# The 48-row group of up products moved to the front in a stage of eight experts, and ScalarE's loop over the experts written out

## What is computed

```python
gate_up = jnp.einsum('ecd,edm->ecm', buf, w_up_gate)
gate, up = jnp.split(gate_up, [I], axis=-1)          # I = 176
h = jax.nn.silu(gate) * up
out_buf = jnp.einsum('eci,eid->ecd', h, w_down)
```

## Time and profile before

| | us |
|---|---|
| median of 3 runs | 791.88 |
| lowest and highest | 791.78, 792.73 |
| the profiled execution | 792.51 |
| its span, in which all profile times lie | 790.5 |
| PE, DVE, ACT, POOL busy | 739.8, 574.6, 467.8, 544.3 |

### The profile page before, as it was taken

The page is one execution under the profiler, slowest core; times in us unless marked ns, Lnnn a source line. Parts: engine busy times, 40 slices in busy tenths (PEclk is TensorE's granted clock), DMA queues, the critical chain, the costliest instruction groups (busy, mean ns, idle before and its releaser), DMA issues.

```text
span 790.5 us, 14041 instructions
## 1 busy us (share of the span) xinstructions
PE 739.8 (94%) x4364; PEld 628.5 (80%) x4364; DVE 574.6 (73%) x1539; ACT 467.8 (59%) x1163; POOL 544.3 (69%) x459
## 2 busy tenths in 40 slices
PE   5799999999999999999999999999899989899993
PEld 4587788888888888888777888777778879888882
DVE  6976886777777766868887777988754447777577
ACT  5567776676666676765666766665633246554262
POOL 4466998787878887777888888778534253431773
PEclk9999999999999999999999999999999999999997
DMA  9411245422222212222222221212142035441352
GB/s 299 124 53 54 84 158 180 156 72 72 63 68 66 74 61 69 62 67 58 65 65 83 82 80 61 63 58 64 48 152 71 34 139 199 176 166 67 88 149 84
DMA packets 47748, 75.73 MB, mean 96 GB/s; under 512 B 9728, under 2 KB 24640, under 8 KB 47680
## 3 DMA queue, kind: packets, MB, share of 16 engines
q1 hardware_dynamic: 43504, 65.19, 26.6%
q0 software_dynamic: 3072, 8.39, 3.4%
q10 hardware_dynamic: 1104, 1.31, 0.5%
HBM read 57.71 MB, written 17.17 MB: 95 GB/s over the span
## 4 chain that ended last, share of the span: by engine, by line
PE 71%; DVE 11%; issue 8%; ACT 4%; POOL 3%; DMA 2%; DVEq 0%; ACTq 0%; POOLq 0%
PE ps L433 20%; PE ps L969 16%; PE ps L934 13%; PE ps L985 9%; PE ps L955 7%; PE ps L1133 3%; POOL got L1883 1%; DVE q_sw L1315 1%; DVE q_sw L1314 1%; DVE hid_both L1646 1%; POOL slot_inputs L1790 1%; DVE hid_hi L1636 1%; POOL o_lo L1774 1%; DVE hid L1641 1%; DVE hid L1633 1%
## 5 line engine op out<-in xcount | busy, mean ns | idle before, releaser
L969 PE MATMUL ps<-pt,vp 128*128 128x512 f32 (+3 forms) x512 | 149.5, 434 | 10.3 <-DVE q_sw L1315 10.0
L634 ACT ACTIVATE prob<-ps,neg_max 128x512 f32<-128x512 f32 (+3 forms) x256 | 132.6, 525 | 34.7 <-DVE neg_max L1324 30.6
L969 PEld LDWEIGHTS ps<-pt,vp 128*128 128x128 f32 x512 | 82.7, 190 | 59.9 <-issue 30.5
L1324 DVE CUSTOM_DVE_ANT_0 ps<-ps,causal_row 128x512 f32<-128x512 f32 (+3 forms) x256 | 120.1, 511 | 5.5 <-PE ps L934 5.4
L1755 POOL TENSOR_TENSOR q_sw<-q_cos,q_sw 128x512 f32<-128x512 f32 x62 | 79.2, 1277 | 64.4 <-DVE q_cos L1316 64.3
L643 ACT ACTIVATE pt<-ps,vcol 128x512 f32<-128x512 f32 x64 | 44.1, 690 | 109.5 <-PE ps L955 109.5
L1774 POOL TENSOR_TENSOR o_lo<-o_t,o_hi 128x512 fp32r<-128x512 f32 x64 | 84.3, 1317 | 33.4 <-ACT o_hi L672 33.4
L955 PE MATMUL ps<-id_f,prob 128*128 128x128 f32 x640 | 92.3, 275 | 0.9 <-ACT pt L643 0.9
L934 PE MATMUL ps<-k_hi,q_hi 128*128 128x512 f32 x248 | 87.1, 351 | 0.4 <-POOL q_lo L1759 0.3
L1759 POOL TENSOR_TENSOR q_lo<-q_sw,q_hi 128x512 fp32r<-128x512 f32 x62 | 80.2, 1293 | 4.0 <-ACT q_hi L666 3.6
L1343 DVE TENSOR_TENSOR o_t<-ps,inv_row 128x512 f32<-128x512 f32 x64 | 44.3, 692 | 52.5 <-PE ps L969 52.5
(11 more groups left out here) (220 smaller groups left out, 1940.2 us busy)
## 6 DMA issues: line engine op xcount, KB each, us to landing
kh_row<-kvh_rows SPq DMA_DIRECT2D x64, 256.0 KB, 3.2
inv_row<-inverse_sums SPq DMA_DIRECT2D x64, 256.0 KB, 3.2
slot_inputs<-zeros SPq DMA_DIRECT2D x8, 640.0 KB, 4.9
xg<-slot_inputs SPq DMA_DIRECT2D x8, 640.0 KB, 4.5
slot_outputs<-yo SPq DMA_DIRECT2D x8, 640.0 KB, 3.3
up_raw<-in_w_up_dram SPq DMA_DIRECT2D x8, 368.0 KB, 4.8
wo_raw<-in_wout_dram SPq DMA_DIRECT2D x4, 512.0 KB, 7.9
dn_sb<-in_w_dn_dram SPq DMA_DIRECT2D x8, 256.0 KB, 3.7
```

Source lines behind the costliest of these rows:

```text
L634: ins = act.activation(prob[:, i % 2, ROW_AT[nt]:ROW_AT[nt] + w], ps_s[bank][:, at:at + w], ACT.Exp, scale=-1.0, bias=neg_max[:, i % 2, nt ...
L969: ins = pe.matmul(ps_qo[:, mt * P:SEQ], vp[:, b * TPB + mt, :], pt[:, i % 2, cols], start=(mt == 0), stop=(mt == PT_BANKS[-1][-1]))
L1324: ins = dve.tensor_tensor_reduce(s_, s_, causal_row[:, (NT - 1 - nt) * P:], 1.0, BIG, ALU.add, ALU.min, neg_max[:, i % 2, nt:nt + 1])
```

## The change

On TensorE, group 2 goes ahead of groups 0 and 1. TensorE now waits for the first count of `gu_free` ahead of group 2 and for the second ahead of group 0. On ScalarE `sg2` is made before `sg`. On VectorE the 48-row chain goes ahead of the 128-row chain. ScalarE's loop of three passes is written out into straight code; the other engines keep their loops.

```diff
@@ ScalarE, expert_steps
-                        act.activation(sg[:, c, :], ps[3][:, 0:HC], ACT.Silu).then_inc(silu_ready, 1)
-                        act.wait_ge(gu_psum, 3 * (2 * e + c) + 3)
                         act.activation(sg2[0:H2, c, :], ps[5][0:H2, 0:HC], ACT.Silu).then_inc(silu_ready, 1)
+                        act.wait_ge(gu_psum, 3 * (2 * e + c) + 2)
+                        act.activation(sg[:, c, :], ps[3][:, 0:HC], ACT.Silu).then_inc(silu_ready, 1)
@@ ScalarE, the loop
-            with act.Fori(0, NE // 2 - 1) as pair:
-                expert_steps(pair * 2, False)
-            expert_steps(NE - 2, True)
+            for e in range(0, NE, 2):
+                expert_steps(e, e == NE - 2)
@@ TensorE, expert_up
-                for k, (a, z) in enumerate(((0, P), (P, 2 * P), (2 * P, UPW))):
+                for k, a, z in ((2, 2 * P, UPW), (0, 0, P), (1, P, 2 * P)):
+                    if k == 2:
+                        pe.wait_ge(gu_free, 2 * m + 1)
                     if k == 0:
-                        pe.wait_ge(gu_free, 2 * m + 1)
-                    if k == 2:
                         pe.wait_ge(gu_free, 2 * m + 2)
```

More of the change, by code:

```diff
@@ L817, in expert_steps @@
                         act.wait_ge(gu_psum, 3 * (2 * e + c) + 1)
+                        act.activation(sg2[0:H2, c, :], ps[5][0:H2, 0:HC], ACT.Silu).then_inc(silu_ready, 1)
+                        act.wait_ge(gu_psum, 3 * (2 * e + c) + 2)
                         act.activation(sg[:, c, :], ps[3][:, 0:HC], ACT.Silu).then_inc(silu_ready, 1)
-                        act.wait_ge(gu_psum, 3 * (2 * e + c) + 3)
-                        act.activation(sg2[0:H2, c, :], ps[5][0:H2, 0:HC], ACT.Silu).then_inc(silu_ready, 1)
                         if c == 0:
@@ L1631, in expert_steps @@
                         dve.wait_ge(silu_ready, 2 * m + 1)
-                        dve.wait_ge(gu_psum, 3 * m + 2)
+                        dve.tensor_tensor(hid2[0:H2, c, :], sg2[0:H2, c, :], ps[5][64:64 + H2, 0:HC],
+                                          ALU.mult).then_inc(gu_free, 1)
+                        dve.wait_ge(gu_free, 2 * m + 3)
+                        dve.tensor_copy(hid2_both[0:H2, cs], hid2[0:H2, c, :]).then_inc(hid_hi_ready, 1)
+                        dve.wait_ge(hid_hi_ready, 2 * m + 1)
+                        dve.tensor_tensor(hid2_both[LO:LO + H2, cs], hid2[0:H2, c, :],
+                                          hid2_both[0:H2, cs].bitcast(F32), ALU.subtract).then_inc(hid_ready, 1)
+                        dve.wait_ge(silu_ready, 2 * m + 2)
+                        dve.wait_ge(gu_psum, 3 * m + 3)
                         dve.tensor_tensor(hid[:, c, :], sg[:, c, :], ps[4][:, 0:HC], ALU.mult).then_inc(gu_free, 1)
-                        dve.wait_ge(gu_free, 2 * m + 3)
+                        dve.wait_ge(gu_free, 2 * m + 4)
                         dve.tensor_copy(hid_hi[:, cs], hid[:, c, :]).then_inc(hid_hi_ready, 1)
-                        dve.wait_ge(hid_hi_ready, 2 * m + 1)
+                        dve.wait_ge(hid_hi_ready, 2 * m + 2)
                         dve.tensor_tensor(hid_lo[:, cs], hid[:, c, :], hid_hi[:, cs].bitcast(F32),
                                           ALU.subtract).then_inc(hid_ready, 1)
[L1640 to L1647, removed]
                     if not (last and r == 1):
```

## The result

The changed kernel takes 784.07 us in the median of 5 runs (783.76 to 784.89). The kernel before, run on the same chip, takes 792.37 us (791.78 to 792.92, 5 runs). The ratio is 0.990, with a 95% interval of 0.9886 to 0.9913: faster by 8.3 us. The forecast was 785.4 us.

What follows compares the result with a forecast made beforehand. VectorE's chain was taken to set the expert stage's pace through TensorE's waits. Gains summed over eight experts gave -6.4 or -6.5 us, from the median of 791.88 to 785.4 us; own range 784.0 to 786.4, wider range 784.0 to 790.8.

Steps and rivals of the forecast that it cites:

- TensorE's wait for VectorE: TensorE stops once in each of eight experts, before the second bank of down products, for VectorE's half-1 subtraction; 5.5 us.
- The table loads: ScalarE in the expert stage: two of three loads go, in experts 2 and 4, worth 0.92 us each.
- The exchange and the margin of 0.04: Half 0: VectorE's 128-row cast at 3.47, GpSimd's L1863 at 3.51, VectorE first; half 1 begins 1.29 behind the cast.
- GpSimd first: Rival, half 0: cast comes behind GpSimd, half 1 begins 0.64 later; 790.4 us; 0.20, shared with loop's change doing all.
- Port held longer: Rival, half 0: VectorE's subtraction waits until L1863's recorded end, 0.30 later; 787.7 us; 0.12, with only some experts won.
- Single experts: Lengths: experts 0, 2, 4 at 9.94 us; 1, 3, 5, 6 at 9.5; TensorE's resume in expert 7 at B + 7.56.
- Experts 2 and 4: End of half 1: GpSimd's up-weight split still meets VectorE's last subtraction, which takes 0.97; each expert 9.94 for 11.47 us.
- The new wait on TensorE: Group 0 of half 1 waits for half 0's 128-row multiplication; 0 to 0.1 us, 0.1 taken, only where VectorE isn't last.

Runs made afterwards that it cites:

- late_cast320: Changed kernel with a 48x320 memset on VectorE between the 128-row multiplication and its cast in half 0 of every expert; 789.17 us.
- loads_first: Changed kernel with SyncE issuing the load of the up weights ahead of the load of the slots; 787.05 us.
- split_wait: Changed kernel with GpSimd's split of the next expert's up weights waiting for VectorE's last subtraction (hid_ready); 784.15 us.
- late_cast: Changed kernel with a 128x6 memset on VectorE between the 128-row multiplication and the cast of half 0; 785.02 us.
- late_cast96: Changed kernel with a 128x96 memset on VectorE between the 128-row multiplication and the cast of half 0; 784.85 us.
- late_sub: Changed kernel with a 128x6 memset on VectorE behind the subtraction of half 0; 785.12 us.
- split_wait_loads: Changed kernel with GpSimd's up-weight split waiting for VectorE's last subtraction and SyncE loading up weights ahead of slots; 784.63 us.
- exchange: Changed kernel with ScalarE's loop put back, so only the new order of the groups; 786.81 us.

## Why the prediction was right

**TensorE's wait for VectorE** (right). It was the thing to shorten: 5.5 us became 1.3, and the stage lost 6.72 us where the sum had 6.45. "TensorE stops once in each of the eight experts" leaves out the other three stops of before (1.2 us together, shown above); the sum holds nonetheless, since it goes by the lengths of whole experts.

**The table loads** (right in kind). One load in the stage instead of three; alone 2.2 us of the stage against 1.84, but 1.40 and 0.78 in experts 2 and 4 instead of 0.92 each.

**The exchange and the margin of 0.04** (right). The cast was forecast at 0.04 ahead of GpSimd and is 0.03 ahead. The forecast hung on that, and the rival *GpSimd first* had a mechanism that exists: expert 2 shows it, and late_cast320, with GpSimd first everywhere, gives 789.17 us where the rival had 790.4. It has a memset of its own, so the likeness of the two times proves little; the step of 1.89 or 1.90 from GpSimd's start to half 1 does, which is the rival's 1.89. *Port held longer* did not happen: half 1 begins 1.31 behind the cast, not 1.59. The SBUF page of the Trainium skill ("SBUF — State Buffer", section "SBUF: two separate sides") has the pair locked for the whole instruction. In late_cast320 the cast ended at 657.82 and needs 0.33, so it began at 657.49, 0.14 before the recorded end of GpSimd's instruction at 657.63: the same 0.14 as in the earlier trace rows. The runs don't tell whether the port or the record ends early.

**Single experts.** Forecast and measured lengths: expert 0, 9.94 and 9.96; experts 1, 3, 5 and 6, 9.5 and 9.48 or 9.49; the resume in expert 7 at B + 7.56 and B + 7.60. The measured lengths of experts 0 to 6 are from `sg2` to `sg2`.

**Experts 2 and 4** (wrong step, of small size). "In experts 0, 2 and 4 GpSimd starts that split 0.13 behind the multiplication" and "that stays as it is, moved along": it stayed in expert 0 alone. "SyncE's loads and stores ... move with the experts" failed with it. I moved VectorE's chain and TensorE forward and left the DMA where it was relative to them. With everything else earlier, the up weights are what comes last before the split: it waited for them in five experts instead of three, 14.0 us instead of 6.2. In expert 4 the split came at 689.75, behind a subtraction that had started at 688.94 and took 0.49; the expert was 9.51, 0.43 better than forecast. In expert 2 the same lateness did harm from the other side, by the lost race, and the expert was 10.12, 0.18 worse. Its stop of 0.29 looks like the one of about 0.3 that was forecast there, but by luck, since its last subtraction took 0.49. It is luck too that the two misses are of opposite sign. loads_first and split_wait show that the place of the split decides how long the last subtraction takes: 0.97 or 0.49.

**The new wait on TensorE** (0 to 0.1 forecast, 0.1 taken; the size is right). Group 0 of half 1 waited for the same multiplication in the kernel before; the exchange made it later. In expert 1 the step behind the first matmul of half 1 is 0.22 instead of 0.15, so 0.07. In expert 2, with `hid` 0.12 late, the group started 0.09 late and the step behind it was 0.25: 0.19 in all, 0.12 more than in expert 1. That, the stop of 0.45 (0.29 shown, and 0.16 hidden in the matmul before) and 0.03 for the slower first matmul behind it make 0.60 of the 0.61 from first matmul to first matmul (0.64 from `sg2` to `sg2`).

**The size.** The profiled executions differ by 7.6 us, the medians of five by 8.3. The sum was made against the profiled one. Of the difference of 1.3 between the forecast and the median, 0.3 comes from the stage. No run explains the rest. It is as large as the spread of the medians of programs whose experts run alike, 784.07 to 785.12.

## What to carry to other kernels

When two engines ask for a shared port within some hundredths of a microsecond, write down the start of both after the change: here the cast led by 0.03 us, and the two orders lay 0.6 us apart in an expert, and which of them leads is set by the order of steps on a third engine. After a speed-up look again at who is last at each wait, the transfers above all; a transfer that was in time before may be last now, and that may help (it kept GpSimd out of the way) or harm. And add to a shown stop of TensorE what the modelled length of the matmul before it hides, 0.16 us here, before you speak of slack.

## What the runs showed of the hardware

**A small instruction can be free on VectorE, by its place.** From one instruction to a dependent one there are 0.03 us beyond the first's length, and memsets of 0.06 and 0.14 us on other data between a multiplication and its cast did not move the cast (late_cast, late_cast96). One of 0.33 us set it back by 0.43. Behind the subtraction, that of 0.06 us cost 0.01 at most (late_sub), that of 0.14 cost 0.09 and that of 0.33 again 0.43. The memset of 0.33 us was not stretched although GpSimd's down-rest had begun 0.07 ahead of it; the cast behind it was.

**TensorE's clock at the start of the stage.** In three of fourteen profiled executions (the repeated changed kernel, loads_first and split_wait_loads) the first microseconds of expert 0 ran at the lower of TensorE's two levels. Busy times by stretch, with the granted clock as third number from the end, of split_wait_loads and then of split_wait:

```profile
644.00:646.00 2.00, 2.00 (x9) 2.00 (x9) 0.00 (x0) 0.62 (x2) 0.00 (x0) 0.51 0.65 264
646.00:648.00 2.00, 2.00 (x11) 2.00 (x10) 1.29 (x3) 0.83 (x4) 0.00 (x0) 0.64 0.00 0
```

```profile
644.00:646.00 2.00, 2.00 (x15) 2.00 (x15) 0.74 (x2) 0.83 (x4) 0.00 (x0) 1.00 0.94 370
646.00:648.00 2.00, 2.00 (x15) 1.91 (x14) 1.86 (x5) 1.50 (x5) 0.84 (x1) 1.00 0.20 80
```

0.51 is the 1.2 GHz level, 1.00 the 2.4 GHz one. In both the engine had just stood still for 1.60 us, waiting for `xg_lo`, so the stop alone doesn't decide it. The matmuls came 0.27 us apart instead of 0.15, and the first 128-row multiplication of VectorE began 4.46 us behind the stage's start instead of 3.02: 1.44 us. In loads_first and split_wait_loads the cast of expert 0 came behind GpSimd as well and took 0.85 and 0.86, which is the other half of a microsecond. Six runs of split_wait_loads fall into 783.72 to 785.05 (four) and 786.78 and 786.87 (two, the profiled one among them); that the clock parts them was not shown, since only the profiled one has a trace. The mean granted clock over a whole run doesn't part them either: 0.988 and 0.989 in the two, 0.987 to 0.992 in the four. What makes it fall in some executions stays open.

**A table load with no drain to be seen.** The page "ScalarE: Activation LUTs" of the Trainium skill (section "What ACT_TABLE_LOAD costs") gives 1283 ns for the load, as the trace has it (1.28), and 1380 ns more for a drain, in each switch to a different set of tables. In exchange the load starts 0.02 us behind the end of the copy before it (662.74 + 0.37 to 663.13), and the silu 0.01 behind the load's end (663.13 + 1.28 to 664.42), so no such time is to be seen on either side. Whether these loads switch to a different set, no run tells.
